# First expert blocks of three experts as plain fp32 matmuls inside the routing steps of a graph-attention and mixture-of-experts kernel

## The reference

```python
h = layernorm(x)                                   # per token, 128 features
Wh = h @ W
e = leaky_relu(Wh @ a[:128] + (Wh @ a[128:]).T)    # per graph, 64 x 64, masked by adj
x = x + elu(softmax(e) @ Wh)
g = layernorm(x)                                   # the "second norm"
scores = g @ Wg.T + bg                             # 8 experts
top2, probs = softmax over the two best scores
for e in range(8):
    y = relu(g @ W1[e].T + b1[e]) @ W2[e].T + b2[e]   # 128 -> 512 -> 128
    out += combine[e] * y
return x + out
```

## Time and profile before

| what | value |
|---|---|
| median of 3 runs | 448.1 us (447.94 to 448.4) |
| profiled execution, its own time | 447.63 us |
| span of its profile, first to last instruction | 445.5 us |
| mean granted clock of PE | 0.974 of full speed |
| PE busy | 407.9 us |
| DVE busy | 359.0 us |
| ACT busy | 320.3 us |
| POOL busy | 285.0 us |

### The profile page before, as it was taken

How to read it: one execution, slowest core, us unless ns; L and a number is a source line. 1 busy time by engine, 2 the same in 40 slices (tenths; PEclk the granted TensorE clock), 3 DMA queues, 4 the chain that set the end, 5 groups by cost and what they waited for, 6 DMA issues and landing times.

```text
span 445.5 us, 9041 instructions
## 1 busy us (share of the span) xinstructions
PE 407.9 (92%) x2231; PEld 308.6 (69%) x2246; DVE 359.0 (81%) x1410; ACT 320.3 (72%) x760; POOL 285.0 (64%) x292
## 2 busy tenths in 40 slices
PE   7888898889999888899999999999999999999990
PEld 3656666666666666688888877877887878878630
DVE  6679999999998899789888687696886777677863
ACT  2677887888888898478897677677777768768500
POOL 1041777777777777677777765666665666766653
PEclk9989999999999999599999999999999999999995
DMA  6996334333333344443532332332322342388799
GB/s 166 273 380 217 106 115 121 110 96 103 103 102 103 96 126 120 128 110 122 169 101 73 101 119 85 89 107 89 89 89 85 89 119 59 96 267 264 239 310 323
DMA packets 56291, 63.03 MB, mean 141 GB/s; under 512 B 7744, under 2 KB 40896, under 8 KB 56000
## 3 DMA queue, kind: packets, MB, share of 16 engines
q1 hardware_dynamic: 35728, 33.28, 25.5%
q0 software_dynamic: 9344, 20.10, 13.4%
q10 hardware_dynamic: 11184, 9.26, 6.9%
HBM read 27.28 MB, written 26.94 MB: 122 GB/s over the span
## 4 chain that ended last, share of the span: by engine, by line
PE 61%; DVE 22%; ACT 6%; issue 5%; DMA 3%; ACTq 1%; SPq 1%; POOL 0%; DVEq 0%; POOLq 0%
PE bank L1447 7%; PE bank L1444 7%; PE bank L1445 7%; PE bank L1431 7%; PE bank L1435 7%; PE bank L1432 7%; PE bank L1415 3%; PE bank L1423 3%; PE bank L1391 3%; PE bank L1393 3%; DVE xn L1060 2%; DVE bn L895 2%; DVE score L1037 2%; DVE neg_max L1042 2%; DVE x_all L885 2%
## 5 line engine op out<-in xcount | busy, mean ns | idle before, releaser
L508 POOL DMA_INDIRECT expert_slots<-rows,slot_i x128 | 126.6, 989 | 54.5 <-issue 37.8
L1444 PE MATMUL bank<-hh,w_hi 128*128 128x512 f32 x144 | 61.3, 426 | 0.0
L1431 PE MATMUL bank<-xh,w_hi 128*128 128x512 f32 x144 | 59.7, 415 | 1.5 <-ACT xh L685 1.2
L700 ACT ACTIVATE yb<-bank,b_sb 128x512 f32<-128x512 f32 x36 | 24.8, 688 | 49.3 <-PE bank L1447 49.3
L1447 PE MATMUL bank<-hl,w_hi 128*128 128x512 f32 x144 | 58.2, 404 | 0.3
L1445 PE MATMUL bank<-hh,w_lo 128*128 128x512 f32 x144 | 58.1, 403 | 0.0
L1435 PE MATMUL bank<-xl,w_hi 128*128 128x512 f32 x144 | 57.5, 399 | 0.2 <-DVE xl L1112 0.2
L1432 PE MATMUL bank<-xh,w_lo 128*128 128x512 f32 x144 | 57.3, 398 | 0.0
L1136 DVE CAST hh<-z 128x512 fp32r<-128x512 f32 x36 | 16.7, 464 | 47.7 <-ACT z L690 47.6
L524 POOL DMA_INDIRECT moe_rows<-hexp,ysi x40 | 40.3, 1007 | 20.2 <-issue 10.6
L524 POOL DMA_INDIRECT moe_rows<-hrelu,ysi x40 | 40.0, 1000 | 17.4 <-issue 10.7
(11 more groups left out here) (166 smaller groups left out, 1044.7 us busy)
## 6 DMA issues: line engine op xcount, KB each, us to landing
rows<-xn SPq DMA_DIRECT2D x32, 256.0 KB
xs<-expert_slots SPq DMA_DIRECT2D x27, 260.0 KB
x_all<-x SPq DMA_DIRECT2D x16, 256.0 KB, 3.6
w_raw<-w_t SPq DMA_DIRECT2D x2, 2048.0 KB, 13.7
w_raw<-moe_rows SPq DMA_DIRECT2D x16, 256.0 KB, 4.1
out<-x_all ACTq DMA_DIRECT2D x16, 256.0 KB, 5.0
xs<-expert_slots ACTq DMA_DIRECT2D x11, 260.0 KB
w_hi<-moe_rows SPq DMA_DIRECT2D x9, 256.0 KB, 3.7
```

Of the source, the lines that this page charges most:

```text
L508: nc.gpsimd.indirect_dma_start(out=slots, out_offset=bass.IndirectOffsetOnAxis(ap=slot_i[q][:, k * SUB + j:k * SUB + j + 1], axis=0), in_= ...
L700: nc.scalar.activation(yb[:, :], ps_y[:, :], ACT.Identity, bias=b2_sb[:, e:e + 1]).then_inc(yb_ok, 1)
L1431: nc.tensor.matmul(ps_h[c][:, :], w1_hi[:, e, chunk], xh[:, :], start=True, stop=False)
L1444: nc.tensor.matmul(ps_y[:, :], w2_hi[:, e, c, :], hh[:, c, :], start=c == 0, stop=False)
```

## The change

Experts 4 to 6 get an "early" block each (EARLY = 3): the first 512 rows of each, which are taken as complete after five groups (a floor of 512 on their counts after group 5, and three more padded regions). These three blocks run inside routing steps 9 to 16, spread over four steps each, two steps apart: in step 9 + 2k SP has loaded the rows into `xs` and PE turns them (early_x); in the next step come two hidden chunks; in the one after that two more hidden chunks and the first two results; then the last two results. They are plain fp32 matmuls, with no high and low parts: eight a block instead of 24. They stand in the place of fills, which are left out where they stand. ACT copies the turned rows, makes four relus and one bias addition per block; the block's result stays in SBUF. PE turns the three results ahead of blocks 2, 3 and 4 of the expert phase (early_turn), DVE weighs them (weigh_early) and POOL scatters them (send_early) behind the second, third and fourth quadruple. The table takes one block off each of the three experts, and QUADS falls from 7 to 6.

The second norm is written by ACT straight into the first half of the row buffer; there are three such buffers instead of two and no xn2 buffers. SP copies the first half into the second with one DMA a group; for groups 0 and 1 ACT makes that copy itself (second_set).

High halves of experts 0 and 1 move to steps 6 and 7, low halves to steps 7 and 8 (the raw weights of experts 0 and 1 then hold early results); low halves of experts 4 to 7 are made behind blocks 5, 7, 9 and 11 instead of 7, 11, 15 and 19. The gate's result moves into the bank of the ranks, so the gate matmuls also wait for the count before.

```diff
+RING = 3
+TURNED = 2
-QUADS = 7
+QUADS = 6
+EARLY = 3
+EARLY_GROUPS = 5
+EARLY_STEP = 9
-HIGH, LOW = 14, 15
+HIGH, LOW = 6, 7
...
+        def early_at(t, first):
+            k = (t - first) // 2
+            return k if (t - first) % 2 == 0 and 0 <= k < EARLY else None
...
         # SP
+            def pass_on(g):
+                sp.wait_ge(xn2_ok, SUB * g + SUB)
+                if g > TURNED:
+                    sp.wait_ge(rowx_ok, 16 * (g - TURNED))
+                sp.dma_start(rows[g % RING][:, 1, :, 0:D], rows[g % RING][:, 0, :, 0:D]).then_inc(rowx_ok, 16)
+            def load_early(k):
+                if k == 0:
+                    for g in range(EARLY_GROUPS - RING, EARLY_GROUPS):
+                        dispatched(sp, g)
+                else:
+                    sp.wait_ge(xe_ps, k)
+                    sp.wait_ge(mete_ok, k)
+                sp.dma_start(xs[:, :, :], slots[early_row(k):early_row(k) + GROUP, :].rearrange("(p s) r -> p s r", s=SUB)
+                             ).then_inc(xe_in, 16)
+            for g in range(TURNED, SURE_GROUPS + 2):
+                pass_on(g)
+                if early_at(g, EARLY_STEP - 3) is not None:
+                    load_early(early_at(g, EARLY_STEP - 3))
...
         # POOL
+            for m in range(EARLY + 1):
                 for b in range(BUFS):
                     send_rows(BUFS * m + b, b)
+                if m > 0:
+                    send_early(m - 1)
+            with pool.Fori(EARLY + 1, QUADS) as m:
+                for b in range(BUFS):
+                    send_rows(BUFS * m + b, b)
+            pool.wait_ge(sent_e, 16 * SUB * EARLY)
...
         # ACT
-            def second_norm(gx, q):
+            def second_norm(gx):
                 act.wait_ge(shift_ok, gx + 1)
-                if later(gx - 1):
-                    act.wait_ge(rowx_ok, 32 * (gx - 1))
+                if gx >= RING:
+                    dispatched(act, gx - RING)
                 for j in range(SUB):
-                    nc.scalar.activation(xn2[q][:, j, :], x_all[:, bass.ds(gx, 1), j, :].rearrange("p g d -> p (g d)"), ACT.Identity, bias=shift[:, j:j + 1],
+                    nc.scalar.activation(rows[gx % RING][:, 0, j, 0:D], x_all[:, bass.ds(gx, 1), j, :].rearrange("p g d -> p (g d)"), ACT.Identity, bias=shift[:, j:j + 1],
+            def second_set(gx):
+                act.wait_ge(xn2_ok, SUB * (gx + 1))
+                nc.scalar.copy(rows[gx % RING][:, 1, :, 0:D], rows[gx % RING][:, 0, :, 0:D]).then_inc(rowa_ok, 1)
+            def early_relu(k, c, tile):
+                act.wait_ge(he_ps, HC * k + c + 1)
+                nc.scalar.activation(he[c], tile[:, :], ACT.Relu, bias=b1_sb[:, SURE + k, c:c + 1]).then_inc(re_ok, 1)
...
             def step(t, groups, q, m):
+                k_x, k_even, k_odd = (early_at(t, EARLY_STEP + n) for n in range(3))
                     softmax_exp(g1)
+                if early_at(t, EARLY_STEP + 3) is not None:
+                    early_out(early_at(t, EARLY_STEP + 3))
+                if k_odd is not None:
+                    early_relu(k_odd, 1, ps_av)
...
                     gap_exp(gl)
+                if k_odd is not None:
+                    early_relu(k_odd, 2, ps_t3)
                 if g1 is not None:
                     elu_relu(g1)
                     elu_exp(g1)
+                if k_odd is not None:
+                    early_relu(k_odd, 3, ps_early)
...
                     nc.scalar.copy(wh[:, :, :], tiles(ps_wh)).then_inc(wh_ok, 1)
+                if k_x is not None:
+                    early_x(k_x)
+                if k_even is not None:
+                    early_relu(k_even, 0, ps_t1)
                 if gx is not None:
                     turned_norm(gx)
+                    if gx < TURNED:
+                        second_set(gx)
...
         # DVE
+            def weigh_early(k):
+                dve.wait_ge(yte_ps, k + 1)
+                nc.vector.tensor_tensor(ye[k].rearrange("p (s d) -> p s d", s=SUB), tiles(ps_setup),
+                                        meta_e[:, k, :, 0][:, :, None].to_broadcast([P, SUB, D]), ALU.mult)
+                nc.vector.tensor_copy(ysi_e[:, k, :], meta_e[:, k, :, 1].bitcast(I32)).then_inc(yse_ok, 1)
...
                 if b > 1:
                     low_halves(b)
                 turn(b, b, 0)
+                weigh_early(b - 1)
...
-            with dve.Fori(1, BUFS + 1) as m:
+            with dve.Fori(1, 3) as m:
                 for b in range(BUFS):
                     turn(BUFS * m + b, b, m)
-                low_halves(m + 3)
-            with dve.Fori(BUFS + 1, QUADS) as m:
+                    if b % 2:
+                        low_halves(2 * m + (2 + b // 2))
+            with dve.Fori(3, QUADS) as m:
...
         # PE
             def gates(gx):
+                    pe.wait_ge(count_ok, gx)
...
             def step(t, groups, q, m):
+                k_x, k_even, k_odd, k_out = (early_at(t, EARLY_STEP + n) for n in range(4))
+                if k_odd is not None:
+                    pe.wait_ge(xn2_t_ok, gx)
+                    early_hidden(k_odd, 2, ps_t3)
+                    if k_odd:
+                        pe.wait_ge(ye_ok, k_odd)
+                    early_hidden(k_odd, 3, ps_early)
+                elif k_out is not None:
+                    early_result(k_out, 2)
+                    early_result(k_out, 3)
+                elif g1 is not None:
+                    if later(g1):
+                        pe.wait_ge(prob_t_ok, g1)
+                    fill(ps_tp, FILL_STEP)
                 if g1 is not None:
                     prob_turns(g1)
...
-                    fill(ps_t3, FILL_NORM)
-                    norm_turns(gx, q)
-                    gates(gx, ps_gate)
+                    if k_x is not None:
+                        early_x(k_x)
+                    if k_even is not None:
+                        early_hidden(k_even, 0, ps_t1)
+                        pe.wait_ge(hexp_ok, g1 + 1)
+                        early_hidden(k_even, 1, ps_av)
+                    if k_odd is not None:
+                        early_result(k_odd, 0)
+                        early_result(k_odd, 1)
+                    if k_even is None and k_odd is None:
+                        fill(ps_t3, FILL_NORM)
+                    norm_turns(gx)
+                    gates(gx)
...
             def drain():
+                early_result(EARLY - 1, 2)
+                early_result(EARLY - 1, 3)
                 prob_turns(last)
...
+            for i in range(2, 4):
+                early_turn(i - 2)
+                pe.wait_ge(lo_ok, 2)
+                expert_block(i, 1)
+            early_turn(EARLY - 1)
-            for e in range(1, SURE):
+            for e in range(2, SURE):
```

More of the change, by code:

```diff
@@ L154, in gnn_moe_kernel @@
         u = sb("u", [P, SUB, D])
-        xn2 = [sb(f"xn2_{q}", [P, SUB, D]) for q in range(2)]
-        rows = [sb(f"rows{q}", [P, 2, SUB, ROW]) for q in range(2)]
+        rows = [sb(f"rows{r}", [P, 2, SUB, ROW]) for r in range(RING)]
         xn2_t = sb("xn2_t", [P, GROUP])
@@ L328, in gnn_moe_kernel @@
         stood = sem("stood")
+        xe_in = sem("xe_in")
+        xe_ps = sem("xe_ps")
+        xe_ok = sem("xe_ok")
+        he_ps = sem("he_ps")
+        re_ok = sem("re_ok")
+        ye_ps = sem("ye_ps")
+        ye_ok = sem("ye_ok")
+        mete_ok = sem("mete_ok")
+        yte_ps = sem("yte_ps")
+        yse_ok = sem("yse_ok")
+        sent_e = sem("sent_e")
         sum_ok = sem("sum_ok")
@@ L643, in turned_norm, with early_x, early_out @@
                 nc.scalar.copy(xn2_t[:, :], ps_t3[:, :]).then_inc(xn2_t_ok, 1)
+            def early_x(k):
+                act.wait_ge(lo_ok, 2)
+                act.wait_ge(xe_ps, k + 1)
+                nc.scalar.copy(xe, ps_t1[:, :]).then_inc(xe_ok, 1)
+            def early_relu(k, c, tile):
+                if k == 0 and c == 0:
+                    act.wait_ge(c_b, 32)
+                act.wait_ge(he_ps, HC * k + c + 1)
+                nc.scalar.activation(he[c], tile[:, :], ACT.Relu, bias=b1_sb[:, SURE + k, c:c + 1]).then_inc(re_ok, 1)
+            def early_out(k):
+                act.wait_ge(ye_ps, k + 1)
+                nc.scalar.activation(ye[k], ps_early[:, :], ACT.Identity, bias=b2_sb[:, SURE + k:SURE + k + 1]).then_inc(ye_ok, 1)
             def step(t, groups, q, m):
                 g0, g1, gx, gl, _ = groups
+                k_x, k_even, k_odd = (early_at(t, EARLY_STEP + n) for n in range(3))
                 if isinstance(t, int) and t == 0:
@@ L1184, in drain @@
                 add_bases(last - 2)
[L1185 removed]
+                write_slots(last - 2)
                 keep_meta(0)
@@ L1362, in gates, with early_x, early_hidden, early_result @@
                 for j in range(SUB):
-                    last = nc.tensor.matmul(tile[:, j * E:(j + 1) * E], xn2_t[:, j * P:(j + 1) * P], wg_sb[:, :],
```

(33 more changed lines are left out.)

237 lines of the change are left out of this document (124 added, 113 removed).

## The result

The changed kernel took 445.71 us (median; 442.67 to 448.36), the kernel before on the same chip 448.74 us (446.05 to 450.49): ratio 0.9938, 95% interval 0.9917 to 0.9959, so 2.8 us faster (1.8 to 3.7). Two of its twenty executions, at 518 and 1002 us, lie far above all others and are left out of the range and the ratio. The forecast was 443.8, with a range of 435 to 451, and faster. The profiled execution took 445.81, its span 444.0 against 445.5: 1.5 us less where the sum had 4.3. So the sign came and, by the ratio, two thirds of the size (by these two profiles one third), but not every term of the sum.

The account below looks back on a forecast made before the run. Bounds: a ring of ACT, PE and DVE in the routing, PE alone in the expert phase. Terms -19.4 + 2.4 + 1.0 + 9.2 + 2.5 = -4.3 on the profiled 447.63 give 443.3, as median 443.8 us; range 435 to 451.

Parts of the forecast that it names:

- Three blocks, -19.4: Expert phase: the table falls from 36 blocks to 33, three blocks at 6.46 us each, -19.4 us.
- What follows the last block, 0: End of the kernel: what follows the last block keeps its due times counted from the end, so it is unchanged.
- The last of my signs of failing: Expert phase: POOL, with 36 sends still to make after a later end of the routing, holds DVE's weighing.
- Low halves, +2.4: Steps 7 and 8: DVE's subtractions for experts 0 and 1 cost 1.2 us each; nothing given back in steps 15, 16.
- Second set, +1.0: Groups 0 and 1: ACT's copy at the step's end costs 0.48 each, +1.0, or 0 if steps 3 and 4 had room.
- Early matmuls, +9.2: Steps 9 to 16 and the drain: early blocks' matmuls, transposes and relus add 9.2 us, bounds 0.9 to 19.2.
- The walk over ACT: Routing steps 9 to 15: delays followed through ACT's four waits, +1.73 in steps 11 and 13, +1.29 in 12 and 14.
- Early turns, +2.5: Blocks 2 to 4: twelve transposes, 1.3, and PE waits for DVE's weighing of 0.4 and 0.8; together +2.5 us.
- ACT takes it in: Rival, routing steps: early matmuls fall into ACT's waits and cost 0.9 instead of 9.2, giving 435.5 us; chance 0.17.
- The clock falls in the early steps: Rival, early steps: PE's clock falls to 0.50, 3.8 us a stretch, two stretches giving 451.4 us; chance 0.13.
- Everything in sequence: Rival, early steps: PE and ACT wait for each other's new work, costing 19.2, total 453.8 us; chance 0.10.
- The blocks do not go away: Rival, expert phase: the table still gives 36 blocks, some 463 us; chance 0.03.

Follow-up runs that it names:

- the first experiment: The changed kernel with the odd block in a place of its own behind the six loops, leaving one block for the rest: 442.57 us, ratio 0.9861.
- the three variants: The changed kernel without relus, matmuls, or both, of early blocks' hidden chunks 2 and 3: steps 13 and 14 take 22.68, 22.68 and 21.86 us.

## Why the prediction came out as it did

**Three blocks, -19.4: nearly.** The loops ran 33 blocks (33 bias additions of yb in the trace), with intervals mostly of 6.42 to 6.46 inside the experts. The stretch gained 18.23. Of the 1.2 us missing, 1.0 are the stretched intervals of 7.80 and 7.25 against 7.04 and 7.01 before; for the 7.80 the cause is the late turn at the change of expert, for the 7.25 it is not shown. I had read one interval and taken the loops' shape as given.

**What follows the last block, 0: the step that failed.** I wrote that it keeps its due times counted from the end and left it unchanged. The reads' due times were not what made it longer (the first experiment's rival); the buffers were: two blocks in a row in `u`, and a wait of 3.02 us for the first one's scatter. It cost 3.4 in the profile, and the odd block in its own place gave back 2.6 there and 3.5 by the ratios. The last of my signs of failing, POOL's sends holding DVE's weighing, came about here, though for the shared buffer and not for a later end of the routing. The count that decides, 33 = 24 + 6 + 2 + 1 against 36 = 28 + 6 + 1 + 1, could be worked out from the table's numbers, which I had.

**Low halves, +2.4: right where they went,** 2.05, **not where they came from.** I gave nothing back there. The run without early blocks and with seven loops takes 9.89 and 9.89 in steps 14 and 15 against 10.11 and 10.10 before, and 7.24 against 7.53 from there to the first x-transposes: 0.7 us less where the halves no longer stand (the ring of row buffers is new there too). **Second set, +1.0: too much,** 0.1: I had its lower end at 0 "if steps 3 and 4 had room", and ACT's waits at the end of a step are that room; so a copy of 0.48 behind a wait of 0.46 was the row to go by. POOL's first dispatch starts no earlier, for it now waits for the pads, which stand ahead of it on its own queue; it is the row that answers to the earlier trace rows:

```profile
43.86 1.04 POOL L549 DMA_INDIRECT expert_slots<-rows,slot_i  x1 [14.02 <-DMA expert_slots<-pad_rows]
```

**Early matmuls, +9.2: right in kind, 7.7,** or 8.4 without the 0.7 that the halves give back in the same steps. The walk over ACT had 11.89 and 11.45 for odd and even steps; they are 11.61 and 11.18, some 0.27 less each, in all of them. It also had ACT ready at 127.05 and PE at 127.12 at the end of an odd step, that is, level, which is what the three variants show for the second pair. The 0.27 are a wait that I had kept. Behind the attention PE runs the ranks, whose weights come from DVE's choice; PE's weight loads of the kernel before, then of the changed one:

```profile
119.95 0.10 PEld L1340 LDWEIGHTS bank<-chosen_b,before_b 128*128 128x128 bf16 x1 [0.28 <-DVE chosen_b L959]
```

```profile
145.90 0.10 PEld L1451 LDWEIGHTS bank<-chosen_b,before_b 128*128 128x128 bf16 x1
```

The wait, 0.27 or 0.28, stands in eleven steps of the kernel before and in none of the steps 10 to 15 of the changed one. Where PE's front is longer, DVE's choice is ready in time, and a step pays 0.28 less than the matmuls add. The run without early blocks agrees: its steps 14 and 15 lack that wait as well and take 9.89, and 11.61 and 11.18 are 1.72 and 1.29 more, where the walk had +1.73 and +1.29. So the walk's additions were right, and the step that they were added to was too long.

**Early turns, +2.5: too little, 3.5.** Two waits of 0.97 and 0.93, where I had 0.4 and 0.8. The second came out; in the first, I let PE lose 0.44 for the turn ahead and left DVE where it was, while DVE's turn depends on the same PE and moved with it (its weighing starts 3.05 us behind the x-transposes before and 3.06 after); its copy of the ids took 0.33 and not 0.15.

**The rivals.** *ACT takes it in* (0.9 for 9.2): no (and all four of ACT's waits in the earlier trace rows are for PE, not three, as I wrote there); the early matmuls cost 7.7, and without two of ACT's relus the two pairs of steps are shorter by only 0.11 and 0.12 us. *The clock falls in the early steps:* no; 1.00 from 40 to 188 us. By the rule of the Trainium skill (TensorE: Matmul & The Clock Gate, section A second HAM failure mode: psum-queue depth-cycling) that short idles between groups of matmuls can make the clock swing, these steps were the candidates; the trace does not agree there, with waits of 0.24 to 0.79 in a step at a clock of 1.00. *Everything in sequence:* 19.2 against 7.7. *The blocks do not go away:* refuted by the 33.

So the forecast was near by luck in part: two errors work against each other, 2.8 us too much cost in the routing and 5.6 too little behind it (1.0, 1.2 and 3.4).

## What to carry to other kernels

When a change alters how many times a loop runs, write down the new split into full rounds, pairs and rest, and look at what the remainder shares: a buffer used twice in a row at the very end waits for the scatter of its first use (3.02 us here), and a special ordering tied to a loop's first round moves with it. In a ring of engines, judge an edit by pairs of steps, not by one, and take work away from both sides separately and together before saying which engine is the bound. And where TensorE waits in a short transition, look at its granted clock in the stretch behind: here it cost 3.3 us behind waits of 3.2 us in all.

## What the hardware showed that I had not expected

The fall of the clock in the drain is neither certain nor tied to a single wait. In the run without the relus, whose drain has the same instructions on PE and waits of 0.82, 1.18 and 1.28 us at the same places, the clock stayed at 1.00 and the x-transposes of block 2 followed those of block 1 after 11.23 us; in the changed kernel it was 0.50, the 1.2 GHz level, for some 10 us, and they followed after 14.51. Of the seven profiles of the changed kernel and its variants with early blocks and without fills, six have the longer interval (14.12 to 14.54). The difference of 3.3 us is about as much as the change is worth. That executions of one program differ by it too is not shown by a profile, but their clocks fit: over eighteen executions of the changed kernel the mean granted clock goes from 0.962 to 0.987, and the execution with the lowest is the slowest (448.36 us), that with the highest the fastest (442.67). Sixteen matmuls that nobody reads, in three waits of PE (0.82, 1.18 and 1.21 us in the changed kernel), kept the clock at 1.00 in that stretch in each of the three profiles that have them.
